# Node places of the own side as bf16, made on the chip once, in a graph kernel that gathers 412,500 edges

## The reference, cut to what matters

```python
theta = x[dst] - x[src]
w = sigmoid(relu(theta @ W1 + b1) @ W2 + b2)
agg = segment_sum(w * theta, dst)
indeg = segment_sum(ones, dst)
x = layernorm(x + agg + indeg * (x @ W4 + b4))
```

## Time and profile before

| what | value |
|---|---|
| median of three runs | 4060.63 us |
| span of the profiled execution | 4675.2 us |
| GpSimd busy in it | 3065.3 us |
| VectorE busy | 2941.1 us |
| TensorE matmul busy | 1880.8 us |
| ScalarE busy | 1239.7 us |
| moved by DMA | 695.58 MB, 149 GB/s on average |

### The profile page before, as it was taken

One profiled execution on the slowest core, in us unless ns is written; L12 is line 12 of the kernel. 1 busy time (PEld: TensorE's weight loads), 2 busy tenths in 40 slices (PEclk: granted clock), 3 DMA queues, 4 the chain that ended last, 5 costly groups with the idle time before them and its releaser, 6 DMA issues.

```text
span 4675.2 us, 42596 instructions
## 1 busy us (share of the span) xinstructions
PE 1880.8 (40%) x10770; PEld 1685.0 (36%) x10770; DVE 2941.1 (63%) x4884; ACT 1239.7 (27%) x2269; POOL 3065.3 (66%) x3229
## 2 busy tenths in 40 slices
PE   2134444434344443443444334343444443443433
PEld 2133333334333333343434333333343333333333
DVE  2057666666666666676766666676666666756666
ACT  0122222222222222232222222222222222222221
POOL 6666666666666666666666666666666666666664
PEclk6556666666666666666666666666666666666666
DMA  6445544455545544554444445455554555544453
GB/s 176 145 137 154 152 149 146 150 146 152 150 148 151 149 145 153 146 158 149 150 149 151 146 149 151 146 152 159 150 149 149 150 150 150 156 142 144 150 159 95
DMA packets 347140, 695.58 MB, mean 149 GB/s; under 512 B 128517, under 2 KB 216875, under 8 KB 346639
## 3 DMA queue, kind: packets, MB, share of 16 engines
q0 software_dynamic: 152352, 413.02, 31.0%
q10 hardware_dynamic: 44965, 214.31, 13.4%
q1 hardware_dynamic: 149578, 65.51, 5.4%
HBM read 667.32 MB, written 31.64 MB: 150 GB/s over the span
## 4 chain that ended last, share of the span: by engine, by line
DVE 33%; another core or an unknown queue 28%; issue 27%; ACT 6%; PE 3%; ACTq 1%; DMA 0%; POOL 0%; DVEq 0%; SPq 0%; POOLq 0%
DVE diff L746 7%; DVE logit L754 7%; DVE ps_z L740 6%; DVE scaled_x L769 3%; DVE hot_en L759 3%; ACT away L652 2%; PE ps_sum L602 2%; ACT hot_ne L660 1%; ACTq L435 1%; DVE square L722 1%; ACT ps_log L667 1%; DVE rstd L724 1%; ACT scaled_x L669 1%; DVE carry_sel L794 1%
## 5 line engine op out<-in xcount | busy, mean ns | idle before, releaser
L574 POOL DMA_INDIRECT arena<-table,src_at x3076 | 2925.3, 951 | 1505.7 <-issue 879.8
L602 PE MATMUL ps_sum<-scaled_x,hot_en 128*128 128x130 f32 x6446 | 1300.0, 371 | 596.5 <-issue 488.3
L602 PEld LDWEIGHTS ps_sum<-scaled_x,hot_en 128*128 128x128 f32 x6446 | 1218.8, 282 | 650.8 <-issue 641.6
L740 DVE TENSOR_TENSOR ps_z<-ps_z,arena 128x896 f32<-128x896 f32 x440 | 482.4, 1096 | 717.5 <-remote 594.0
L769 DVE TENSOR_TENSOR scaled_x<-arena,ps_log 128x896 f32<-128x896 f32 x440 | 478.1, 1087 | 544.7 <-ACT ps_log L667 359.5
L660 ACT ACTIVATE hot_ne<-away,ones_col 126x896 bf16<-126x896 bf16 x461 | 479.8, 1041 | 965.8 <-remote 848.5
L585 PE MATMUL ps_z<-parts,hot_ne 126*128 126x128 bf16 x3223 | 385.0, 270 | 784.9 <-issue 729.8
L585 PEld LDWEIGHTS ps_z<-parts,hot_ne 126*128 126x128 bf16 x3223 | 294.2, 124 | 873.9 <-issue 793.5
L593 PE MATMUL ps_sum<-sums,carry_sel 128*128 128x130 f32 x228 | 87.9, 489 | 1188.9 <-DVE sums L775 996.8
L667 ACT ACTIVATE ps_log<-logit,b_col 128x7 f32<-128x7 f32 x461 | 124.9, 271 | 1523.6 <-issue 807.6
L746 DVE SCALAR_TENSOR_TENSOR diff<-ps_z,w_rows 128x896 f32<-128x896 f32 x461 | 502.7, 1090 | 15.8
(11 more groups left out here) (86 smaller groups left out, 984.9 us busy)
## 6 DMA issues: line engine op xcount, KB each, us to landing
dst_rows<-in_dst ACTq DMA_DIRECT2D x230, 882.0 KB
arena<-table,src_at POOLq DMA_INDIRECT x3076
parts<-parts_of SPq DMA_DIRECT2D x461, 31.5 KB
parts_of<-stage SPq DMA_DIRECT2D x115, 96.0 KB
winT<-in_x_cols SPq DMA_DIRECT2D x115, 64.0 KB
window<-in_x SPq DMA_DIRECT2D x115, 64.0 KB
out<-yout SPq DMA_DIRECT2D x115, 64.0 KB
arena<-in_x_turned SPq DMA_DIRECT2D x25, 250.0 KB
```

The source lines that it names most:

```text
L574: nc.gpsimd.indirect_dma_start(gath[:, slot_of(g) + t, :], None, table, ids)\
L602: last = nc.tensor.matmul(ps_sum[:, 0:SW], hot_en[:, b, t, :], scaled_x[:, b, t, :], start=(g == 0 and t == 0), stop=(stop and t == tiles_ ...
L740: v.tensor_tensor(ps_z[b][:, 0:n, :], ps_z[b][:, 0:n, :], u, ALU.subtract).then_inc(z_read, 1)
```

## The change

The destination numbers are turned, once, into places within the chunk's window (destination minus the chunk's base), stored as bf16 in DRAM (`rel_of`), and `dst_rows` is loaded from there. For this:

- SP loads `dst` a second time, one chunk of 3584 numbers for each of 115 partitions (`dst_lin`), and the last 340 numbers (`dst_tail`), ahead of the first group loads. The buffers borrow the room of the last six held batches.
- VectorE (`place_rows`, between `place_bases` and `place_rel`) subtracts the base, on 115 partitions by 3584 numbers and on the tail. In `place_bases` two additions go, since the bias of `distance` no longer holds the base.
- ScalarE's queue stores the places after group 6, and after group 21 waits for that store and then loads the first two `dst_rows`, which had been loaded at the very start.
- GpSimd waits for that store before held block h = 15.
- Each of the 230 loads of `dst_rows` has 2-byte numbers in place of 4-byte ones.

```diff
+LIN_AT = HELD - 4
+REL_AT = LIN_AT - 2
...
-        dst_rows = sb("dst_rows", [P, 2, DB * BATCH], I32)
+        dst_rows = sb("dst_rows", [P, 2, DB * BATCH], BF16)
...
-            v.tensor_tensor(by_chunk(neg_ids, NB), by_chunk(near_off, NB), spread_over(base_f, c, NB), ALU.add)
-            link(v.tensor_tensor(neg_ids[:, n:n + 1], near_off[:, n:n + 1], base_f[:, c - 1:c], ALU.add))
-            v.tensor_scalar(neg_ids[:, :], neg_ids[:, :], node_no[:, :], -1.0, ALU.add, ALU.mult).then_inc(base_ready, 1)
+            v.tensor_scalar(neg_ids[:, :], near_off[:, :], node_no[:, :], -1.0, ALU.add, ALU.mult).then_inc(base_ready, 1)
...
+        def place_rows(dve):
+            v = nc.vector
+            c, left = z.chunks, z.left
+            dve.wait_ge(dst_lin_in, 16 * 2)
+            v.tensor_scalar(base_col[0:c, :], dst_lin[0:c, 0:1], z.last_base, None, ALU.min).then_inc(base_col_ready, 1)
+            dve.wait_ge(base_col_ready, 1)
+            v.tensor_scalar(rel_tail[:, 0:left], dst_tail[:, 0:left], base_f[0:1, c - 1:c], None, ALU.subtract)\
+                .then_inc(rel_lin_ready, 1)
+            v.tensor_scalar(rel_lin[0:c, :], dst_lin[0:c, :], base_col[0:c, :], None, ALU.subtract)\
+                .then_inc(rel_lin_ready, 1)
...
+            full = z.chunks * CHUNK
+            by_chunk_dst = dst[0:full].rearrange("(c e) -> c e", e=CHUNK)
+            for to, what in ((dst_tail[:, 0:z.left], dst[full:z.edges].rearrange("(a e) -> a e", a=1)),
+                             (dst_lin[0:z.chunks, :], by_chunk_dst)):
+                sp.dma_start(to, what).then_inc(dst_lin_in, 16)
             for k in range(COLS):
                 load_group(sp, k)
...
+                if h == REL_AT:
+                    pool.wait_ge(rel_of_out, 16 * 2)
                     pool.sem_inc(pool_gate, 1)
...
-                                    dst[lo:hi].rearrange("(a e) -> a e", a=1).to_broadcast([WK, hi - lo]))\
+                                    rel_of[lo:hi].rearrange("(a e) -> a e", a=1).to_broadcast([WK, hi - lo]))\
...
-            for p in range(2):
-                load_dst_rows(p)
+            def store_rows():
+                full = z.chunks * CHUNK
+                act.wait_ge(rel_lin_ready, 2)
+                act.sem_inc(act_gate, 1)
+                nc.scalar.dma_start(rel_of[0:full].rearrange("(c e) -> c e", e=CHUNK), rel_lin[0:z.chunks, :])\
+                    .then_inc(rel_of_out, 16)
+                nc.scalar.dma_start(rel_of[full:z.edges].rearrange("(a e) -> a e", a=1), rel_tail[:, 0:z.left])\
+                    .then_inc(rel_of_out, 16)
+
             for k in range(z.groups):
                 copy_group(act, k)
+                if k == z.groups // 4:
+                    store_rows()
+                if k == z.groups // 2 + 9:
+                    act.wait_ge(rel_of_out, 16 * 2)
+                    act.sem_inc(act_gate, 1)
+                    for p in range(2):
+                        load_dst_rows(p)
...
             place_bases(dve)
+            place_rows(dve)
             place_rel(dve)
```

More of the change, by code:

```diff
@@ L117, in build @@
         table = nc.dram_tensor("table", (z.nodes, 2 * F), FP32, kind="Internal").ap()
+        rel_of = nc.dram_tensor("rel_of", (z.edges,), BF16, kind="Internal").ap()
         parts_of = nc.dram_tensor("parts_of", (SLOTS, 3 * P, F), BF16, kind="Internal").ap()
@@ L150, in build @@
         held_xT = sb("held_xT", [P, 2, P])
-        dst_rows = sb("dst_rows", [P, 2, DB * BATCH], I32)
+        dst_rows = sb("dst_rows", [P, 2, DB * BATCH], BF16)
+        base_col = sb("base_col", [P, 1])
+        dst_tail = sb("dst_tail", [1, BATCH], I32)
+        rel_tail = sb("rel_tail", [1, BATCH], BF16)
+        dst_lin = held_x[:, LIN_AT * BT:HELD * BT, :].rearrange("p t f -> p (t f)").bitcast(I32)
+        rel_lin = held_x[:, REL_AT * BT:LIN_AT * BT, :].rearrange("p t f -> p (t f)").bitcast(BF16)
+        assert z.chunks <= P and dst_lin.shape[1] == CHUNK and rel_lin.shape[1] == CHUNK
         parts = sb("parts", [P, 2 * NB, F], BF16)
@@ L266, in build @@
         held_in = sem("held_in")
+        dst_lin_in = sem("dst_lin_in")
+        base_col_ready = sem("base_col_ready")
+        rel_lin_ready = sem("rel_lin_ready")
+        rel_of_out = sem("rel_of_out")
         heldT_ready = sem("heldT_ready")
@@ L555, in windows_gpsimd @@
                     pool.wait_ge(src_in[h], 16 if h < EARLY else 16 * (EARLY + 1))
+                    pool.sem_inc(pool_gate, 1)
+                if h == REL_AT:
+                    pool.wait_ge(rel_of_out, 16 * 2)
                     pool.sem_inc(pool_gate, 1)
```

## The result

The changed kernel takes 4069.22 us (13 runs, 4067.79 to 4070.24), the kernel before 4060.60 us (13 runs): 8.6 us more. The ratio is 1.0020, with a 95% interval of 1.0013 to 1.0027. On one chip the kernel before took 4061 us at one time and 4705 at another, and the forms of after differed likewise, for a reason that stays open, so only kernels run together are compared.

A forecast was written before the change was run, and what follows sets the result against it. GpSimd's issuing of 3223 indirect DMAs, 1.25 us apart, was taken as the bound. To 4060.6 us it added 3 for `dst_lin` and 1.2 for VectorE's hold, other parts 0: about 4065 us, range 4056 to 4079.

The forecast's parts named there:

- The bound: GpSimd: issuing 3223 indirect DMAs, 1.25 us from start to start, fills the unprofiled time; the sum is 4051 to 4068 us.
- up to 10 us of waits: Unprofiled runs: at most about 10 us of waits, the ceiling of what relief of transfers or other engines can bring.
- The loads at half the bytes: The 230 `dst_rows` loads, 882 KB each to 441 KB: worth 0 to -10 us, taken as 0.
- rival 3: `dst_rows` loads: 3584 B rows move no faster than 7168 B rows, time again 4065 us; 0.77 together with the forecast.
- ScalarE's input type: ScalarE's `distance` reads bf16 in place of int32: no change, from 1029 ns and 1041 ns for the same shape.
- `dst_lin` ahead of the groups: SP's queue in the set-up: the added load delays the index block before the 22nd gather, 3 us within -0.45 to +8.3.
- my worst case: `dst_lin` load at the worst later slice's 131 GB/s: it takes 12.6 us, making the index block 8.3 us later.
- VectorE's hold on GpSimd: `place_rows`: VectorE's 3.9 us subtraction costs GpSimd a third of its duration, 1.2 us, within bounds of 0 and 3.9.
- The sum of the two: Set-up: the 3 us for `dst_lin` and 1.2 us for VectorE's hold were added to 4060.6, about 4065 us.
- The store, the new wait, the pace: Store of the places, GpSimd's wait before h = 15 and the wait for 24 groups: all covered, taken as 0.
- rival 1: Set-up: fourth index block lands 8.3 us late, with VectorE's hold 4073 us, 4078 if groups slip; chance 0.19.
- The profiled span shrinking: Profile of the changed kernel: the span may shrink by hundreds of microseconds, which would say nothing of the runs.

The follow-up runs named there:

- six_gathers: Changed kernel with six gathers in place of seven for every full table batch from the seventh ring place on, 433 left out; 3527.93 us.
- before_again: The kernel before, unchanged, run again for a profile beside its time; 4063.9 us in its one run.
- scalar_only: Changed kernel with the large subtraction on ScalarE, `dst_lin` still loaded as 115 rows at its old place; 4724.33 us, ratio to the kernel before 1.0017.
- lin_late: Changed kernel with the loads of `dst_lin` and `dst_tail` behind the four index blocks on SP's queue; 4711.21 us, ratio to the kernel before 1.0014.
- all_three: Changed kernel with `dst_lin` behind the index blocks, as 112 + 3 partitions, and the subtraction with two tensor inputs; 4713.77 us, ratio to the kernel before 1.0018.
- split_scalar: Changed kernel with `dst_lin` loaded as 112 + 3 partitions and the large subtraction on ScalarE; 4060.66 us, ratio to the kernel before 1.0000.

## Why the prediction was right or wrong

- *The bound.* Right. It was 1.250 us from gather to gather from a stretch without waits, and six_gathers gives 541/433 = 1.250. That the runs hardly wait, read from a sum against a profile 614.6 us too long, holds: before_again has one pause. But that pause, 5.7 us, is part of what I had allowed as up to 10 us of waits that relief could win. No row names a transfer or another engine as its cause, and it stands in every form.
- *The loads at half the bytes, worth 0.* Right; without any of them the main loop is no shorter. The bytes did go, from 695.58 to 594.10 MB by the two pages. Whether each load takes half the time (rival 3) no row shows.
- *ScalarE's input type, 0.* Right, 1028 ns for 1029.
- *`dst_lin` ahead of the groups.* The place was right, a later index block before the 22nd gather, and the size was wrong. I took 3 us within -0.45 to 8.3, because the new load seemed like the old ones. Measured are 7.55 us of wait, near my worst case. The step that failed is "it moves as the old ones did": 115 partitions don't. The load took about 23 us from issue to use, where my worst case had 12.6, and 11 to 12 us as 112 + 3. The index block landed 11.3 us later, beyond my bound of 8.3, because SP came to issue it 15.1 us later. That the wait stayed under 8.3 is luck: VectorE's hold had already taken 2.0 us of it, and I had the block without slack where before_again has about 2 us. That reading came from a pause of 0.45 us in the profile of 4675.2 us, which before_again doesn't have. The Trainium skill (DMA: Bandwidth & Descriptors, "Why a DMA increments its semaphore by 16 and not by 1") has a load spread over the largest number up to 16 that divides the slowest dimension, 5 for 115, 16 for 112. The traces agree with the direction: 23 us against 11 to 12, and a busy share of 0.3 to 0.6 over the 16 engines. How many engines one load used isn't in any row.
- *VectorE's hold on GpSimd.* I took a third of its duration, 1.2 us, from two small operations. For this operation it is the whole duration: 2.0 us for 2.07. The Trainium skill (SBUF — State Buffer, section SBUF: two separate sides) says so of an operation in a two-port mode, and I set its 2 us aside for a row of two small operations. Which mode this one ran in is in no row. The small ones are no measure even of each other: they stretched a gather by 0.28 us in the profile that I read and none in after or before_again. I had also given the operation 3.9 us; it ran at 0.58 ns for each number, not 1.09 as L399 did.
- *The sum of the two.* I added them. In after the start of the 22nd gather moved by 9.5 us, but taking the hold away alone gave at most 0.7 us of that (scalar_only). The landing of the index block sets the place, and what comes before it is hidden.
- *The store, the new wait, the pace.* Right at 0. In after there is no pause before h = 15, at the 106th gather, and none for 24 groups: the pause at 159.88 is one gather later, and before had it.
- *Forecast and rivals.* The forecast was 4065, a change of 4.2 us in the sum. Measured are 4069.2 and a change of 8.6 us, at the edge of the 0.2% that I had as the limit and just beyond the 8.1 us from which I had rival 1 decide. So rival 1, to which I gave 0.19, is what happened, at 8.6 of its 12.2 us; the measured time lies within my range by a sum whose two terms were both too small.
- *The profiled span shrinking.* It did, by 607 us, but not from the change: before_again has no pause in its main loop, and lin_late and the others, which load bf16 rows too, have over 600 us of them. What brings them on is open.

## What to carry to other kernels

Where one engine issues back to back for the whole run, as GpSimd here, cutting bytes elsewhere brought nothing, and the question is whether an edit makes that engine wait once, above all in the set-up: 9.5 us lost there were still lost at the main loop's first gather. A load put ahead of others in a queue is to be priced with its number of partitions, not by bytes alone; a number such as 115 can be split into 112 and 3. A large operation beside a GpSimd that issues gathers cost nothing on ScalarE and nearly its whole length on VectorE, in this kernel. Waits behind one another don't add up, so a second price can hide under the first.

## What the runs showed of the hardware that I had not expected

- 1.65 MB to 115 partitions, first in the queue, were usable 22.4 to 23.1 us after their issue in six profiles, to 112 + 3 partitions after 11.1 to 12.1 us in three. Behind the index blocks it was 28.5 and 29.3 us (lin_late and its repeat) and 17.1 us (all_three).
- Behind the load of 115 partitions SP took 13.6 us to issue eight loads of 250 KB, and behind 112 + 3 partitions 4.1 us (split_scalar); in before_again it was 4.7 us.
- A subtraction of two SBUF tensors on VectorE, 3.87 us, held a gather's issue for 3.65 us, more than the form with one tensor (2.07 us, held for 1.7 to 2.0 us). ScalarE's of the same size, 3.28 us, held it for nothing.
- One pause of 5.6 to 6.6 us beyond the gap stands before GpSimd's 114th indirect DMA in the five profiles whose main loop has no pause, and one of 5.6 to 8.5 us in the nine others; it doesn't move with 14 more instructions ahead of it (one run).
